# The stage between two mixtures of experts: sums on GpSimd, row copies on ScalarE, maxima as bias, attention products on two halves of the array

## The chip, the core and the metric

One core of one Trainium2 chip runs the whole program in one launch. The metric is the device time of that launch in microseconds (us), the median of several runs. One more execution was profiled; its span and its own time are given below. PE is TensorE, DVE is VectorE, ACT is ScalarE, POOL is GpSimd and SP is SyncE.

## What is computed

Four steps over x of 4 batches x 512 tokens x 512 features, all in float32. Only the third and the routing of the fourth lie in the stage that changes:

```python
x = x + L0_xattn(layernorm(x), ctx, ctx)          # 16 heads, 64 keys
x = x + L0_ffn(layernorm(x))                      # latent attention, then 1 shared + 7 routed experts, top 2
x = x + L1_xattn(layernorm(x), ctx, mask)         # one head of 512, 64 keys:
#   scores = x @ ctx.T * 512**-0.5; softmax over the keys that the mask keeps; attn @ ctx; zero if no key is kept
x = x + L1_ffn(layernorm(x))                      # softmax router over 32 experts, top 8, inner size 192
```

## The kernel before

The kernel has six stages, each a block in which the five engines run their own instruction lists and meet only at semaphores: `cross` (the first cross-attention), `front` (the latent attention and the first routing), `mixture` for MOE0, `middle` (from L1834), `mixture` for MOE1, and `finish`. Every engine works through its list in the order in which it is written, so an instruction that waits holds up all behind it on that engine.

`middle` reads the result of the first mixture from two tables in DRAM (`sum` and `other`) and adds them (`add_tables`, L2008). It works by batch (`BATCH` = 4) and in each by tile of 128 tokens (`TPB` = 4). For a batch b it does this:

- VectorE takes the statistics of each tile (`statistics`, L2013 to L2019) and GpSimd the power of -0.5 of the variance (`first_norm`, L1919). VectorE (batch 0, L2025) or ScalarE (L1942) writes the normed rows.
- TensorE flips them (`xn_flips`, L2174), ScalarE copies each flip out of PSUM (L1954), and TensorE makes the scores against the keys (`scores`, L2186).
- `softmax` on VectorE scales and masks the scores, takes the maximum and subtracts it (L2040 to L2043). ScalarE makes the exponents of all four tiles in one instruction (L1958). `shares` sums them, inverts the sum and multiplies (L2047 to L2051).
- `attended`: TensorE transposes the four tiles of 64 columns (L2193), ScalarE copies them (L1962), and TensorE multiplies each with the 64 rows of the context (L2198) into one of two banks of PSUM.
- `residual` on VectorE, tile by tile: it adds the product from PSUM to x (L2057) and takes the statistics of the sum (L2059); then aggregation and variance. The next product but one waits for the sum (`x3`). GpSimd makes the power (`second_norm`, L1923), VectorE the shift (`shift_of_hidden`, L2034), ScalarE the hidden rows (`hidden`, L1948).
- `logits`: TensorE flips the hidden rows, ScalarE copies them (L1968), TensorE multiplies with the router (L2213). VectorE subtracts the maximum (`shift_logits`), ScalarE exponentiates, `choose_experts` marks the eight best (L2076 to L2091).
- `run_keys` on TensorE (L2226, L2227), `run_starts` on VectorE (L2098 to L2101), then sixteen rounds of `pick` (L2107, L2109: the eight largest, then their replacement) and `list_runs` (L2113 to L2117) list the tokens of every expert. GpSimd writes the list to DRAM with four indirect DMAs, each of which waits for the last one (`write_runs`, L307).

The batches overlap by an order written out by hand. VectorE's loop for b runs: run starts and two picks of b-1, the hidden shift of b, seven picks, the softmax of b+1, seven picks and the list of b-1, the shares of b+1, the logits' shift and the choice of b, the residual of b+1. TensorE's loop: flips and scores of b+1, logits of b, two filler products (`keep_busy`, L212, results of no use), the attended products of b+1, the run keys of b. GpSimd's: second norm of b+1, run writes of b. SyncE first issues the loads in this order: context (L1889), the two tables for the first two tiles and for the next two (L1887), mask (L1892), tables of batch 1, router and run constants, tables of batches 2 and 3; then it stores the rows.

## Time and profile before

| what | us |
|---|---|
| median of 3 runs | 1802.04 |
| lowest and highest of them | 1789.2, 1822.32 |
| profiled execution, its own time | 1789.35 |
| its span | 1787.5 |
| PE, DVE, ACT, POOL busy | 1569.0, 1416.7, 1086.9, 793.5 |

### The profile page before, as it was taken

The numbers are of one execution on the slowest core, as the hardware profiler recorded it, in microseconds if no ns is written. First come the engines' busy times: TensorE is split into PE (matmuls) and PEld (weight loads), VectorE is DVE, ScalarE is ACT, GpSimd is POOL, SyncE is SP. The second block draws the span as 40 slices with busy tenths as digits, with TensorE's granted clock in tenths as the row PEclk, the third lists the DMA queues.
The fourth block names the chain that finished last, engine by engine and source line by source line (L and its number), as shares of the span: only waits on it lengthen the run. The fifth ranks groups of instructions, "written<-read, shape, count | busy, mean of one in ns | idle before, by whom it ended". The sixth has DMA issues, their size and how long they took to land. (4 is left out here: it accounts for less than half of the span.)

```text
span 1787.5 us, 34934 instructions
## 1 busy us (share of the span) xinstructions
PE 1569.0 (88%) x8910; PEld 1208.1 (68%) x8911; DVE 1416.7 (79%) x2889; ACT 1086.9 (61%) x2081; POOL 793.5 (44%) x547
## 2 busy tenths in 40 slices
PE   4578899998887899999959938999999999999990
PEld 2546666766564577777737526888888888888880
DVE  6835866867775488888748776999999999999992
ACT  1124644635452477888624316888888888888870
POOL 5010010110303323555410125788888888888871
PEclk9588998999999699999966658999999999999995
DMA  9225427354450644765574314988888889998768
GB/s 330 96 57 126 111 63 184 77 117 97 95 119 22 177 135 139 174 142 104 83 223 155 119 62 91 221 191 181 198 194 189 190 190 219 222 229 184 130 115 303
DMA packets 169999, 270.58 MB, mean 151 GB/s; under 512 B 20416, under 2 KB 96192, under 8 KB 168192
## 3 DMA queue, kind: packets, MB, share of 16 engines
q0 software_dynamic: 49008, 117.24, 32.7%
q1 hardware_dynamic: 120896, 152.18, 29.3%
q8 instruction: 46, 0.75, 0.2%
q14 instruction: 49, 0.40, 0.1%
HBM read 153.72 MB, written 89.06 MB: 136 GB/s over the span
## 5 line engine op out<-in xcount | busy, mean ns | idle before, releaser
L1662 DVE TENSOR_TENSOR moe_w_lo<-moe_w_up,moe_w_hi 128x1536 fp32r<-128x1536 f32 (+1 forms) x216 | 408.2, 1890 | 1.7 <-ACT moe_w_hi L1524 1.7
L1462 POOL DMA_INDIRECT moe_rows<-moe_rows,moe_ids x200 | 326.1, 1631 | 67.4 <-issue 57.9
L1524 ACT ACTIVATE moe_w_hi<-moe_w_up 128x1536 fp32r (+3 forms) x216 | 342.4, 1585 | 0.0
L1766 PE MATMUL psum<-moe_w_hi,moe_rows_hi 128*128 128x384 f32 (+1 forms) x864 | 322.5, 373 | 4.7 <-DVE moe_rows_lo L1656 4.7
L1767 PE MATMUL psum<-moe_w_lo,moe_rows_hi 128*128 128x384 f32 (+1 forms) x864 | 305.9, 354 | 0.0
L1768 PE MATMUL psum<-moe_w_hi,moe_rows_lo 128*128 128x384 f32 (+1 forms) x864 | 305.8, 354 | 0.0
L1776 PE MATMUL psum<-moe_w_down,moe_hid_t 128*128 (+1 forms) x432 | 221.3, 594 | 0.0
L1478 POOL DMA_INDIRECT moe_sum<-moe_res,moe_ids x100 | 163.2, 1632 | 81.3 <-ACT moe_res L1559 43.5
L1478 POOL DMA_INDIRECT moe_other<-moe_res,moe_ids x100 | 165.5, 1655 | 75.8 <-ACT moe_res L1559 33.6
L739 ACT ACTIVATE prob<-psum,neg_top 128x128 f32<-128x128 f32 (+3 forms) x256 | 133.1, 528 | 83.1 <-DVE neg_top L869 78.4
L1766 PEld LDWEIGHTS psum<-moe_w_hi,moe_rows_hi 128*128 128x128 f32 x864 | 163.4, 189 | 13.5 <-DVE moe_rows_lo L1656 5.8
L1768 PEld LDWEIGHTS psum<-moe_w_hi,moe_rows_lo 128*128 128x128 f32 x864 | 163.3, 189 | 9.4
L1767 PEld LDWEIGHTS psum<-moe_w_lo,moe_rows_hi 128*128 128x128 f32 x864 | 163.7, 189 | 7.9
L1656 DVE TENSOR_TENSOR moe_rows_lo<-psum,moe_rows_hi 128x512 fp32r<-128x512 f32 x216 | 149.1, 690 | 12.4 <-ACT moe_rows_hi L1507 6.0
L869 DVE TENSOR_REDUCE neg_top<-psum 128x1 f32<-128x128 f32 (+3 forms) x256 | 117.2, 482 | 50.0 <-PE psum L1093 49.8
L1546 ACT ACTIVATE moe_gate<-psum 128x192 f32<-128x192 f32 (+1 forms) x216 | 74.3, 344 | 134.6 <-PE psum L1768 134.5
L1507 ACT ACTIVATE moe_rows_hi<-psum 128x512 fp32r<-128x512 f32 x216 | 127.2, 589 | 21.7 <-PE psum L1747 21.7
L1134 PE MATMUL psum<-const_sb,prob 128*128 128x128 f32 x640 | 111.2, 289 | 29.7 <-ACT prob L739 26.6
L1747 PE MATMUL psum<-const_sb,moe_rows 128*128 128x128 f32 x864 | 130.0, 273 | 3.6 <-DMA moe_rows<-moe_rows,moe_ids 2.3
L1747 PEld LDWEIGHTS psum<-const_sb,moe_rows 128*128 128x128 f32 x864 | 107.5, 141 | 35.9 <-DMA moe_rows<-moe_rows,moe_ids 3.8
L1779 PE MATMUL psum<-moe_tail_hi,moe_tail_t 128*128 128x512 f32 x160 | 127.2, 795 | 0.0
L293 POOL DMA_INDIRECT moe_slots<-entry,slot x24 | 23.8, 992 | 231.9 <-DVE slot L992 225.5
(295 smaller groups left out, 3117.1 us busy)
## 6 DMA issues: line engine op xcount, KB each, us to landing
moe_w_up<-in_L_ffn_w_gate SPq DMA_DIRECT2D x32, 384.0 KB
moe_w_up<-in_L_ffn_w_up SPq DMA_DIRECT2D x32, 384.0 KB
q_st<-q_hi SPq DMA_DIRECT2D x64, 128.0 KB, 2.9
k_st<-k_hi SPq DMA_DIRECT2D x64, 128.0 KB, 3.0
k_st<-k_lo SPq DMA_DIRECT2D x64, 128.0 KB, 3.2
q_st<-q_lo SPq DMA_DIRECT2D x64, 128.0 KB, 3.0
moe_w_down<-in_L_ffn_w_down SPq DMA_DIRECT2D x32, 256.0 KB
moe_w_down<-in_L_ffn_w_down SPq DMA_DIRECT2D x64, 128.0 KB
```

What stands on the lines that cost most here:

```text
L739: sc.activation(prob[:, u, e, 0:(i + 1) * P], score_at(n, e, (i + 1) * P), ACT.Exp, bias=neg_top[:, u, e:e + 1], accum_out=den[:, i, 2 * h ...
L1462: pool.indirect_dma_start(rows[u][:, :], None, d["rows"], bass.IndirectOffsetOnAxis(ids[:, t:t + 1], 0)).then_inc(gathered[u], 16)
L1478: pool.indirect_dma_start(sums[t % 2], bass.IndirectOffsetOnAxis(ids[:, t:t + 1], 0), res[t % RESULTS][:, :], None, compute_op=ALU.add).th ...
L1507: sc.activation(rows_hi[i][:, :], ps[:, i, :], ACT.Copy).then_inc(T["rth"], 1)
L1524: sc.activation(w_hi[u % SPLITS][:, :], w_up[:, bass.ds(at * DC, DC), :].rearrange("p a n -> p (a n)"), ACT.Copy).then_inc(T["wh"], 1)
L1656: v.tensor_tensor(rows_lo[i][:, :], ps[:, i, :], rows_hi[i][:, :].bitcast(F32), ALU.subtract).then_inc(T["rts"], 1)
L1662: v.tensor_tensor(w_lo[u % SPLITS][:, :], w_up[:, bass.ds(at * DC, DC), :].rearrange("p a n -> p (a n)"), w_hi[u % SPLITS][:, :].bitcast(F ...
L1747: last = tr(ps[:, i, k * P:(k + 1) * P], rows[u][:, k * P:(k + 1) * P], ident)
L1766: mm(ps[:, 2 + i, 0:2 * I], hi, w_h, start=(k == 0), stop=False)
L1767: mm(ps[:, 2 + i, 0:2 * I], hi, w_l, start=False, stop=False)
L1768: last = mm(ps[:, 2 + i, 0:2 * I], lo, w_h, start=False, stop=(k == DC - 1))
L1776: mm(ps[:, 5 + i, :], hid_t[i][:, j, :], tile_at(w_down, at * n_fc + j), start=(j == 0), stop=False)
```

## The change

The sums of the two tables move to GpSimd for batches 1 to 3; batch 0 stays on VectorE, two tiles at a time. The residual sums move to GpSimd too: ScalarE copies each attended product from PSUM to `attended_sb`, and GpSimd adds that. The softmax no longer subtracts the maximum: VectorE writes it negated, and ScalarE takes it as the bias of four exponents, one a tile, which also give the sum. The context is loaded twice, into both halves of the partitions, and behind the first tables; two tiles of shares are transposed at once, so that even tiles lie in partitions 0 to 63 and odd ones in 64 to 127, and their products use the two halves of the array's rows. On VectorE the run starts and four rounds of picks of b come before the residual of b+1, two more behind it. Four semaphores of `front` are used again in `middle` and cleared for that at the start of the first mixture.

```diff
--- before
+++ after
...
+        m["spare_front"] = [S[n] for n in ("z", "zt", "zts", "pp")]
...
+            if moe is MOE0:
+                for used in m["spare_front"]:
+                    pool.sem_clear(used)
...
-        ctx_sb, ctx_t = sb("ctx_sb", [KEYS, BATCH, D]), sb("ctx_t", [P, BATCH, DC, KEYS])
+        ctx_sb, ctx_t = sb("ctx_sb", [P, BATCH, D]), sb("ctx_t", [P, BATCH, DC, KEYS])
...
-        att_t = sb("att_t", [KEYS, TPB, P])
+        att_t = sb("att_t", [P, TPB // 2, P])
+        attended_sb = sb("attended_sb", [P, TPB, D])
...
@@ SyncE @@
-            sp.dma_start(ctx_sb[:, :, :], a["ctx_2048"].rearrange("b k d -> k b d")).then_inc(S["ctx"], 16)
+            sp.dma_start(mask_u8[:, :, :].rearrange("p b k -> p (b k)"), a["mask_BxS2_bk0"].rearrange("b k -> (b k)").partition_broadcast(P)).then_inc(S["mask"], 16)
             tables(0, 2, x_in[0])
             tables(2, 2, x_in[1])
-            sp.dma_start(mask_u8[:, :, :].rearrange("p b k -> p (b k)"), a["mask_BxS2_bk0"].rearrange("b k -> (b k)").partition_broadcast(P)).then_inc(S["mask"], 16)
+            for half in range(2):
+                sp.dma_start(ctx_sb[half * KEYS:(half + 1) * KEYS, :, :], a["ctx_2048"].rearrange("b k d -> k b d")).then_inc(S["ctx"], 16)
@@ GpSimd @@
+            def residual(b):
+                for t in range(TPB):
+                    pool.wait_ge(attended_out, tile(b, t) + 1)
+                    at = x[:, tile(b, t), :]
+                    g.tensor_tensor(at, at, attended_sb[:, t, :], ALU.add).then_inc(S["x3"], 1)
+
             def second_norm(b):
+                residual(b)
                 pool.wait_ge(S["var2"], b + 1)
...
+            def add_tables(b):
+                pool.wait_ge(x_in[b + 1], 32)
+                for n in range(tile(b, 0), tile(b + 1, 0)):
+                    g.tensor_tensor(x[:, n, :], x[:, n, :], x_other[:, n, :], ALU.add).then_inc(added, 1)
+
             first_norm(0)
+            add_tables(1)
             first_norm(1)
+            add_tables(2)
+            add_tables(3)
             second_norm(0)
@@ ScalarE @@
-                act.wait_ge(S["shift"], b + 1)
-                sc.activation(att[:, :, :], att[:, :, :], ACT.Exp).then_inc(S["e"], 1)
+                act.wait_ge(S["ntop"], b + 1)
+                for t in range(TPB):
+                    sc.activation(att[:, t, :], att[:, t, :], ACT.Exp, bias=top[:, t:t + 1], accum_out=den[:, t:t + 1]).then_inc(S["e"], 1)
...
-                sc.activation(att_t[:, :, :].rearrange("p t q -> p (t q)"), ps[0:KEYS, 5, :], ACT.Copy).then_inc(S["pts"], 1)
+                sc.activation(att_t[:, :, :].rearrange("p t q -> p (t q)"), ps[:, 5, 0:TPB // 2 * P], ACT.Copy).then_inc(S["pts"], 1)
+
+            def attended_rows(b):
+                for t in range(TPB):
+                    act.wait_ge(S["o"], tile(b, t) + 1)
+                    since(act, S["x3"], tile(b - 1, t) + 1)
+                    sc.activation(attended_sb[:, t, :], ps[:, 6 + t % 2, :], ACT.Copy).then_inc(attended_out, 1)
...
@@ VectorE @@
+            def add_tables(t):
+
+                if t % 2 == 0:
+                    dve.wait_ge(x_in[t // 2], 32)
+                own.did(v.tensor_tensor(x[:, t, :], x[:, t, :], x_other[:, t, :], ALU.add))
...
+                else:
+                    for t in range(TPB):
+                        dve.wait_ge(added, tile(b - 1, t) + 1)
+                        own.did(v.bn_stats(stats[:, t, :], x[:, tile(b, t), :]))
...
-                own.run(v.tensor_reduce(top[:, :], att[:, :, :], AX.X, ALU.max))
-                v.tensor_tensor(att[:, :, :], att[:, :, :], top[:, :].unsqueeze(2).to_broadcast([P, TPB, KEYS]), ALU.subtract).then_inc(S["shift"], 1)
+                v.tensor_reduce(top[:, :], att[:, :, :], AX.X, ALU.max, negate=True).then_inc(S["ntop"], 1)
...
-                dve.wait_ge(S["e"], b + 1)
-                own.run(v.tensor_reduce(den[:, :], att[:, :, :], AX.X, ALU.add))
+                dve.wait_ge(S["e"], TPB * (b + 1))
...
-                    dve.wait_ge(S["o"], tile(b, t) + 1)
-                    at = x[:, tile(b, t), :]
-                    v.tensor_tensor(at, at, ps[:, 6 + t % 2, :], ALU.add).then_inc(S["x3"], 1)
                     dve.wait_ge(S["x3"], tile(b, t) + 1)
-                    own.did(v.bn_stats(stats2[:, t, :], at))
+                    own.did(v.bn_stats(stats2[:, t, :], x[:, tile(b, t), :]))
...
-                if b > 0:
-                    run_starts(b - 1)
-                    pick(b - 1, range(0, 2))
                 shift_of_hidden(b)
                 if b == 0:
                     statistics(2)
                 else:
-                    pick(b - 1, range(2, 9))
+                    pick(b - 1, range(6, 9))
...
                 shift_logits(b)
                 choose_experts(b)
                 if ahead:
+                    run_starts(b)
+                    pick(b, range(0, 4))
                     residual(b + 1)
+                    pick(b, range(4, 6))
@@ TensorE @@
-                for t in range(TPB):
-                    last = tr(ps[0:KEYS, 5, t * P:(t + 1) * P], att[:, t, :], ident)
+                for j in range(TPB // 2):
+                    last = tr(ps[:, 5, j * P:(j + 1) * P], att[:, 2 * j:2 * j + 2, :].rearrange("p t k -> p (t k)"), ident)
...
-                    since(pe, S["x3"], tile(b, t) - 1)
-                    mm(ps[:, 6 + t % 2, :], att_t[:, t, :], ctx_sb[:, b, :], start=True, stop=True).then_inc(S["o"], 1)
+                    since(pe, attended_out, tile(b, t) - 1)
+                    rows = slice(t % 2 * KEYS, (t % 2 + 1) * KEYS)
+                    mm(ps[:, 6 + t % 2, :], att_t[rows, t // 2, :], ctx_sb[rows, b, :], start=True, stop=True).then_inc(S["o"], 1)
...
-            pe.wait_ge(S["ctx"], 16)
+            pe.wait_ge(S["ctx"], 32)
```

## Rows read from the trace of the kernel before

**Rows 1.** Busy time by stretch of the stage; columns: us, each engine's busy us, PEclk, DMA share, GB/s

```profile
904.17:946.06 41.89, 32.21 (x110) 18.66 (x111) 25.42 (x61) 10.29 (x16) 3.06 (x3) 0.66 0.68 234
946.06:971.38 25.32, 23.18 (x117) 16.01 (x117) 22.27 (x78) 11.30 (x20) 3.02 (x3) 0.77 0.46 139
971.38:1005.25 33.87, 33.19 (x119) 24.36 (x119) 23.81 (x101) 11.76 (x20) 5.01 (x5) 0.51 0.59 185
1005.25:1031.39 26.14, 23.78 (x106) 13.34 (x104) 23.50 (x99) 7.00 (x13) 4.95 (x5) 0.75 0.30 107
1031.39:1060.36 28.97, 11.08 (x53) 9.83 (x52) 24.61 (x121) 5.39 (x9) 3.91 (x4) 0.56 0.16 54
```

**Rows 2.** Timeline of TensorE in the round of 33.9 us: start, duration, engine, line, operation

```profile
960.19 7.19 PE L2198 MATMUL psum<-m_ctx_sb,m_att_t 64*128 64x512 f32 x8 [0.72 <-ACT m_att_t L1962]
...
968.19 3.81 PE L2174 MATMUL psum<-const_sb,m_xn 128*128 128x128 f32 x16
...
971.79 6.93 PE L2186 MATMUL psum<-m_ctx_t,m_xn_t 128*128 128x64 f32 x32
...
988.72 3.68 PE L212 MATMUL psum<-const_sb 128*64 128x512 f32 x4
```

**Rows 3.** Groups of VectorE in the stage: count | busy us, mean ns of one | idle before

```profile
L2107 DVE MAX8 m_picks<-m_left 128x8 f32<-128x128 f32 x60 | 17.6, 294 | 1.9
L2109 DVE MATCH_REPLACE8 m_left<-m_picks,m_left 128x128 f32<-128x128 f32 x56 | 15.4, 275 | 0.0
...
L2059 DVE BATCH_NORM_STATS2 m_stats<-m_x_sb 128x6 f32<-128x512 f32 x16 | 11.1, 694 | 0.6
...
L2057 DVE TENSOR_TENSOR m_x_sb<-m_x_sb,psum 128x512 f32<-128x512 f32 x16 | 10.9, 682 | 5.5 <-PE psum L2198 5.2
...
L2008 DVE TENSOR_TENSOR m_x_sb<-m_x_sb,m_x_other 128x512 f32<-128x512 f32 x16 | 10.1, 686 | 19.6 <-DMA m_x_other<-moe_other 19.6
...
L2047 DVE TENSOR_REDUCE m_den<-m_att 128x4 f32<-128x256 f32 x4 | 1.7, 413 | 2.3 <-ACT m_att L1958 2.3
```

**Rows 4.** Groups of GpSimd and ScalarE by shape: prices of what is moved to them

```profile
L719 POOL TENSOR_TENSOR x_sb<-x_sb,h 128x512 f32<-128x512 f32 x16 | 20.0, 1264 | 202.7 <-DVE h L955 186.3 <-DMA moe_slots<-entry,slot 16.4
...
L739 ACT ACTIVATION_READ_ACCUMULATOR prob<-psum,neg_top 128x1 f32 x256 | 52.2, 204 | 0.0
...
L1954 ACT ACTIVATE m_xn_t<-psum 128x512 f32<-128x512 f32 x16 | 9.4, 597 | 31.8 <-PE psum L2174 31.8
...
L1958 ACT ACTIVATE m_att<-m_att 128x256 f32<-128x256 f32 x4 | 1.7, 415 | 1.8 <-DVE m_att L2043 1.8
```

**Rows 5.** Timeline of the lead-in: context, filler products, table sums, first attended product

```profile
909.33 1.97 PE L2219 MATMUL psum<-const_sb,m_ctx_sb 64*128 64x64 f32 x16 [13.64 <-DMA m_ctx_sb<-in_ctx]
...
911.23 6.77 PE L212 MATMUL psum<-const_sb 128*64 128x512 f32 x10
...
911.88 1.29 DVE L2008 TENSOR_TENSOR m_x_sb<-m_x_sb,m_x_other 128x512 f32<-128x512 f32 x2 [18.16 <-DMA m_x_other<-moe_other]
...
914.59 1.29 DVE L2008 TENSOR_TENSOR m_x_sb<-m_x_sb,m_x_other 128x512 f32<-128x512 f32 x2 [1.41 <-DMA m_x_other<-moe_other]
...
937.33 5.38 PE L2198 MATMUL psum<-m_ctx_sb,m_att_t 64*128 64x512 f32 x8 [0.68 <-ACT m_att_t L1962]
...
938.56 0.69 DVE L2057 TENSOR_TENSOR m_x_sb<-m_x_sb,psum 128x512 f32<-128x512 f32 x1 [0.19 <-PE psum L2198]
```

**Rows 6.** Timeline of GpSimd: first and last of four run writes of batch 0

```profile
986.60 1.05 POOL L307 DMA_INDIRECT moe_slots<-m_run_ids,run_at  x1 [16.05 <-DVE m_run_ids L2117]
...
995.13 0.96 POOL L307 DMA_INDIRECT moe_slots<-m_run_ids,run_at  x1 [1.98 <-DMA moe_slots<-m_run_ids,run_at]
```

**Rows 7.** A line of GpSimd with its shortest, median and longest ns; VectorE's timeline beside it

```profile
L410 POOL TENSOR_TENSOR c_x_rest<-c_x_rest,c_mean x9: 1254/1265/2237, 27.3 to 38.7; 128x512 f32<-128x512 f32 x9
...
36.36 1.23 DVE L474 TENSOR_TENSOR c_att<-c_att,const_sb 128x1024 f32<-128x1024 f32 x1
...
38.88 2.13 DVE L476 TENSOR_TENSOR c_att<-c_att,c_top 128x1024 f32<-128x1024 f32 x1
```

More of the change, by code:

```diff
@@ L1846, in middle @@
         ps, x = m["psum"], sb("x_sb", [P, TILES, D])
[L1847 to L1848 removed]
+        ctx_sb, ctx_t = sb("ctx_sb", [P, BATCH, D]), sb("ctx_t", [P, BATCH, DC, KEYS])
+        N, K, spare = MOE1.routed, MOE1.top, m["spare"] + m["spare_front"]
         w_rt = sb("w_rt", [P, DC, N])
@@ L1871, in middle @@
         run_ids = [sb(f"run_ids{u}", [P, P]) for u in range(BATCH - 1)] + [m["run_ids"]]
-        names = ("w mask ctx ct cts xn ft fe s shift e p pt pts o x3 hn logit lsh le masked ranked "
+        names = ("w mask ctx ct cts xn ft fe s ntop e p pt pts o x3 hn logit lsh le masked ranked "
                  "slotted rows_out own var rstd var2 rstd2 shared runs shift1 shift2").split()
@@ L2117, in list_runs @@
                 v.tensor_tensor(run_ids[b][:, :], found[:, :], empty[:, :], ALU.add).then_inc(S["slotted"], 1)
-            add_tables(0)
-            statistics(0)
-            normed(0)
             dve.wait_ge(S["mask"], 16)
@@ L2126, in _ @@
             own.wait()
-            add_tables(1)
+            statistics(0)
+            normed(0)
             statistics(1)
```

26 lines of the change are left out of this document (11 added, 15 removed).

## Prediction

> **What bounds the kernel now.** I read the busy time by stretch first [rows 1]. The stretch of the change, the stage between the mixtures, is 904.2 to 1060.4, 156 us of the span of 1787.5, so whatever happens there is small against the whole. I cut it where the shift of the second norm of a batch is written (L2034), since everything of the next batch hangs on that point; call it T(b). T(0) to T(3) are 946.06, 971.38, 1005.25 and 1031.39, so there are a lead-in of 41.9 us, rounds of 25.3, 33.9 and 26.1, and a tail of 29.0. The columns to compare are DVE, PE and the clock. In the round of 26.1 DVE works 23.5, and with the gap of some 0.03 after each of its 99 instructions that is all of it: VectorE bounds it. In the round of 33.9 the granted clock is 0.51, the lower level (1.2 GHz), PE is busy 33.2 and DVE only 23.8: there TensorE's own queue is the bound. TensorE's timeline of that round [rows 2] shows that queue: attended products from 960.19 (7.2), then the run keys, flips and scores of the next batch (3.8 and 6.9), flips and logits from 978.5 to 988.8, two filler products (3.7), transposes and a copy, and then the next attended products. So a round is the later of two loops, and the clock decides which.
>
> **The change, part by part.**
> *VectorE.* What goes are twelve of sixteen table sums at 0.686, sixteen residual sums at 0.682, four reductions of 128x256 at 0.413 and four subtractions of that size, put at 0.42 [rows 3]: 8.2 + 10.9 + 1.7 + 1.7 = 22.5 us. Half of it lies in the lead-in and first round. In a later round 2.73 + 0.42 + 0.41 = 3.6 go, and VectorE alone would need 26.1 - 3.6 = 22.5.
> *What takes its place.* A residual row now goes TensorE, ScalarE copy out of PSUM (0.597 for 128x512), GpSimd sum, VectorE statistics (0.694) [rows 3, 4]. The same sum of 128x512 on GpSimd stands in the attention stage: 1.264 [rows 4]. Four in a row are 5.05, and the last statistics come some 0.72 after them. Before, sum and statistics took 1.38 a tile, 5.5 for four: with 1.23 from the first product to what reads it (937.33 to 938.56, [rows 5]) it was 6.7 at the high clock. The new chain is no shorter: 1.23 + 0.65 + 5.05 + 0.72 = 7.65.
> *Exponents.* One of 128x256 at 0.415 becomes four of 128x64 with an accumulated sum. The read of an accumulator is 0.204 [rows 4]; the small exponent itself has no row, it lies between 0.1 (a quarter) and 0.415; I take 0.26, so 4 x (0.26 + 0.204) + gaps = 1.95, 1.5 longer. It sits on ScalarE between the second and third copy of the hidden flips, hence on the path to the logits, partly.
> *Two halves of the array.* Two transposes of 128x128 instead of four with 64 columns, and an att_t copy of half the length: 0.5 less. Products of even and odd tiles use different rows. A pair takes 3.4 at the low clock now; side by side it would take 1.7, one after the other 3.4, and the trace has no pair on row halves. I take side by side: some 2.4 less a batch at the low clock, 1.2 at the high one. The Trainium skill ("TensorEngine Tiling (Array Packing)", Key Properties) says that different tiles of the array run LdWeights and Matmul in parallel; no run shown bears that out for these halves, and by the other end a low round would be about 2 longer.
> *Lead-in.* The context comes last now and twice (1 MB), behind the first two table pairs. Those arrive at 911.88 and 914.59, 1 MB in 2.7 us [rows 5]; without 0.5 MB ahead of them they come 1.35 earlier, and the context at 913.2 + 2.7 = 915.9 instead of 909.3. TensorE's queue is in order: 16 transposes 2.0, ten filler products 6.8 [rows 5], so the flips of batch 0 start at 924.7 though the normed rows come no later than now. Flips and scores are 10.7 at the low clock [rows 2]; the high one gives between half of it and that, I take 7.5: scores at 932.2 (935.4 if low). Softmax without its subtraction 1.4, the load of the exponent's table, unchanged, put at 1.3, exponents 1.95, shares without the reduction 0.9, transposes and copy 0.95: products at 938.7; at the low clock the filler products behind the scores, eight passes of the 0.68 of [rows 5], end at some 942 and put them 3.5 later. GpSimd has its twelve table sums done by about 939.0: batch 1 lands at 921.5 (2 MB more at the rate above), its four sums end 926.6, batches 2 and 3 follow the norm at 928.9 (8 x 1.264). First attended row at 938.7 + 1.23 + 0.65 = 940.6, sums to 945.65, statistics, aggregation and variance 1.3, norm and shift 1.45: T(0) = 948.4, which is 2.3 late.
> *First round.* Hidden rows 3.0, two copies 1.2, exponents 2.0, two copies 1.2, last logits 1.0: 956.8; filler 1.85 (half of the 3.7), transposes, copy: products at 960.0. Now a new wait decides. VectorE goes to the run starts before the residual statistics, and the run keys stand behind the attended products in TensorE's queue. At the high clock they are there at 964.0, else 966.4, while VectorE is through choosing at 961.3. Run starts 0.55 and four rounds of picks (maximum 0.294, replacement 0.275, its load and gaps: 0.72 each, [rows 3]) 2.85, four statistics 2.9, then 0.6 and 1.25: T(1) = 972.1 or 974.5, against 971.38.
> *Later rounds, high clock.* GpSimd's queue decides. The residual sums of batch b+1 stand behind the run writes of batch b-1, four indirect DMAs that each wait for the last one: issued 986.60 to 996.09 [rows 6], 9.5; the chains of the other batches look a little shorter, I take 9.1. Before, only a 1 us power stood behind them. The ids are ready at T + 0.2 + 2.15 + 1.4 + 4.65 + 1.2 = T + 9.6 (three picks, softmax, seven picks, the list). So the writes end at T + 19.0, the sums at 24.05, statistics at 24.8, and with 0.6 and 1.15 the round is 26.5. VectorE's 22.5 is no longer the bound and the round is 0.4 longer, not 3.6 shorter.
> *Later rounds, low clock.* TensorE's loop of 33.9 less 2.4 (pairs) and 0.5 + 0.2 (transposes, copy), plus 1.2 for the wait of the second pair on the copies: about 32.0.
> *Contention.* A GpSimd sum beside a two-input VectorE instruction took 2.237 instead of 1.265, and that instruction (L476) 2.13 where the same size just before (L474) took 1.23 [rows 7]: each pays 0.9. In the residuals GpSimd works beside picks and statistics, which have one SBUF input; only the two softmax operations and the shares of batch 0 meet table sums, with 1 us of slack. I price it at 0 and keep +2 as its end. The Trainium skill ("GPSIMD Engine Reference", the table of the engine's properties) names this contention for VectorE instructions with two SBUF inputs; by the rule the trace agrees, and it would only matter if picks paid it too.
> *Cleared semaphores.* Four more at the start of the first mixture. No row shows a clear. An indirect issue on GpSimd takes 0.96 [rows 6], so four clears lie between 0 and 3.8; I take 0.4, near the lower end, since a clear moves nothing.
>
> **The sum.** With the clock as in this trace (round 1 low, round 2 high, tail unchanged at 29.0): 974.5 + 32.0 + 26.5 + 29.0 = 1062.0, against 1060.4: 1.6 later, and 0.4 makes 2.0. The profiled execution took 1789.35 beside its span of 1787.5, so its like would take 1791.4. The three timed runs stand higher, 1789 to 1822 with median 1802.0; the trace does not show why, and on that scale the sum is 1804.0. I forecast the middle of the two, 1798, which puts no change at 1796. What a measurement of this kernel tells from no change is about 2%, 36 us.
>
> **Rivals.**
> 1. VectorE's 22.5 us come off whole, because every round is VectorE's. For: the busy shares of rounds 0 and 2. Against: the low clock in round 1 and GpSimd's order. Time: 1796 - 22.5 = 1773.5, some 1774. Chance 0.07.
> 2. The clock stays high through the rounds: 972.1 + 2 x 26.5 + 29.0 = 1054.1, 6.3 earlier, less the 0.4: 1790. For: TensorE waits on VectorE less. Against: the five stretches of now stand at 0.51 to 0.77. Chance 0.25.
> 3. Slower: the run keys' wait at the low clock in both rounds. VectorE stands before the residual statistics until TensorE is through its products. It decides where round 2 falls to 1.2 GHz: 974.5 + 64 + 29 = 1067.5, 7.1 later plus 0.4, and 3.5 where the lead-in is low too: 1796 + 11 = 1807. With products one after the other and contention it is 2 x 2 + 2 more, 1813. Chance 0.25.
> 4. The change does not do what it says: pairs serial and four exponents at their upper end (0.62 each, 0.6 more a round than I took, for three rounds, and 2 a round for the pairs): 8 later, 1806. Chance 0.08.
> My forecast has the other 0.35. Every case lies inside 2%; the 0.06 outside is the spread of the runs.
>
> **Range and chances.** The cases span 1774 to 1813, and the runs of one kernel alone differ by 33. I give 1780 to 1818. Over 2% faster would need under 1766, below what even rival 1 gives: 0.03. Over 2% slower, above 1838: 0.03. Within: 0.94.
>
> **What would show it.** Right: the stage from the first context DMA to the end of the last list at 152 to 164 us; VectorE's busy time in it down from 119.6 to about 97, with new idle before the run starts (now L2098) and before the residual statistics; GpSimd sums of 1.26 that begin right behind the fourth run write in batches 2 and 3; flips of batch 0 not before 924. Wrong: statistics that follow the copies at once, context transposes before 914, a stage under 145 or over 170, or a difference that lies outside the stage.

## The result, and the profile after

Four runs of the changed kernel have the median 1818.3 us (1806.6 to 1829.9), beside 1799.6 of four runs of the kernel before. The ratio is 1.0119 [1.0068, 1.017], in brackets the 95% interval: about 21 us slower, 12 to 31. A ratio is estimated from the runs that are not in the chip's slower state, and is not the quotient of the two medians (those differ by 18.7). The prediction, 1798 with 1780 to 1818, said no change; the median lies just above the upper end. The profiled execution took 1818.0 beside its span of 1816.2.

First the busy time by stretch of the changed kernel, cut at the same points as [rows 1] (its stage begins at 916.04, the hidden shift is L2070; us, then PE, PEld, DVE, ACT and POOL busy, PEclk, DMA share, GB/s):

```profile
916.04:965.93 49.89, 27.80 (x131) 16.44 (x131) 20.30 (x47) 13.95 (x28) 23.20 (x19) 0.71 0.65 207
965.93:993.04 27.11, 21.67 (x126) 15.61 (x124) 19.65 (x81) 14.13 (x30) 7.99 (x7) 0.87 0.60 191
993.04:1025.13 32.09, 26.52 (x112) 20.42 (x112) 23.46 (x95) 14.24 (x30) 9.95 (x9) 0.65 0.53 159
1025.13:1057.33 32.20, 20.28 (x74) 13.39 (x73) 23.80 (x93) 9.27 (x22) 9.86 (x9) 0.66 0.21 76
1057.33:1086.64 29.31, 11.51 (x52) 10.89 (x52) 22.02 (x108) 5.39 (x9) 3.90 (x4) 0.50 0.14 47
```

The stage takes 170.6 us, before 156.2. The lead-in is 8.0 longer (49.9 against 41.9), the first round 1.8 longer, the second 1.8 shorter, the third 6.1 longer, the tail 0.3 longer. What follows the stage takes 729.6, before 727.1. The stage also starts 11.9 later, in code that is the same but for four clears; the runs below show that this part moves by itself. So 14.4 of the 28.7 us between the two profiles lie in the stage; against a second execution of the kernel before, whose stage took 146.9 (experiment 5), it is 23.7 longer. A stage over 170, and a difference outside it, were among the signs that I had named of being wrong. Note the DVE column: 109.2 us in the sum, not the 97 that was forecast, though the sums did leave; 7.5 of the 12 are one copy, as the next view shows.

The second view says why; these are groups of VectorE, GpSimd and ScalarE in the stage of the changed kernel (count | busy us, mean ns of one | idle before), to hold against [rows 3, 4]:

```profile
L2138 DVE MAX8 m_picks<-m_left 128x8 f32<-128x128 f32 x60 | 17.6, 294 | 1.8
L2090 DVE BATCH_NORM_STATS2 m_stats<-m_x_sb 128x6 f32<-128x512 f32 x16 | 10.2, 685 | 7.1 <-POOL m_x_sb L1932 7.0
L2130 DVE COPY before<-before 128x32 f32<-128x32 f32 x4 | 8.2, 2046 | 0.0
L2129 DVE COPY m_base<-psum 128x1 f32<-128x1 f32 x4 | 0.6, 158 | 13.5 <-PE psum L2255 13.5
...
L1932 POOL TENSOR_TENSOR m_x_sb<-m_x_sb,m_attended_sb 128x512 f32<-128x512 f32 x16 | 19.8, 1268 | 10.5 <-ACT m_attended_sb L1991 10.5
L1942 POOL TENSOR_TENSOR m_x_sb<-m_x_sb,m_x_other 128x512 f32<-128x512 f32 x12 | 15.1, 1295 | 5.0 <-DMA m_x_other<-moe_other 5.0
...
L1991 ACT ACTIVATE m_attended_sb<-psum 128x512 f32<-128x512 f32 x16 | 8.7, 594 | 9.7 <-PE psum L2226 9.7
L1981 ACT ACTIVATE m_att<-m_att,m_top 128x64 f32<-128x64 f32 x16 | 5.4, 338 | 0.4 <-DVE m_top L2078 0.3
```

A copy of 128x32 has a mean of 2046 ns. Where no sum of GpSimd runs beside it, it takes 0.17 us. And VectorE stands 13.5 us before the line ahead of it, for the run keys. The maxima and statistics have the durations of before, and GpSimd's sums are the 1.26 that [rows 4] showed.

Where that copy stands is plain in the second round, in the timelines of GpSimd and VectorE of the changed kernel (start, us, engine, line):

```profile
1002.41 1.05 POOL L307 DMA_INDIRECT moe_slots<-m_run_ids,run_at  x1 [9.77 <-DVE m_run_ids L2148]
...
1011.50 0.96 POOL L307 DMA_INDIRECT moe_slots<-m_run_ids,run_at  x1 [2.01 <-DMA moe_slots<-m_run_ids,run_at]
1012.49 4.96 POOL L1932 TENSOR_TENSOR m_x_sb<-m_x_sb,m_attended_sb 128x512 f32<-128x512 f32 x4
```

```profile
1008.90 0.29 DVE L2122 TENSOR_TENSOR m_share<-m_share,m_r_total 128x128 f32<-128x128 f32 x1
1013.76 0.16 DVE L2129 COPY m_base<-psum 128x1 f32<-128x1 f32 x1 [4.57 <-PE psum L2255]
1013.84 3.65 DVE L2130 COPY before<-before 128x32 f32<-128x32 f32 x1
1017.53 0.22 DVE L2132 SCALAR_TENSOR_TENSOR run_at<-m_runs,m_base 128x4 int32<-128x4 f32 x1
...
1020.54 2.47 DVE L2090 BATCH_NORM_STATS2 m_stats<-m_x_sb 128x6 f32<-128x512 f32 x4
```

The four residual sums begin right behind the fourth run write, as forecast, and run from 1012.49 to 1017.45. VectorE comes free at 1009.2, waits 4.6 for the run keys, starts its copy (L2130) 1.35 after the sums began, and the copy ends at 1017.49, with the last of them. Only then come four rounds of picks and the statistics, so the shift is written 7.7 after the last sum. In the third round the copy takes 4.14 (from 1045.56), again to the end of the sums.

Last the lead-in of the changed kernel, to hold against [rows 5]:

```profile
923.60 1.29 DVE L2036 TENSOR_TENSOR m_x_sb<-m_x_sb,m_x_other 128x512 f32<-128x512 f32 x2 [1.80 <-DMA m_x_other<-moe_other]
928.47 1.29 DVE L2036 TENSOR_TENSOR m_x_sb<-m_x_sb,m_x_other 128x512 f32<-128x512 f32 x2 [2.25 <-DMA m_x_other<-moe_other]
...
945.27 1.23 DVE L2066 SCALAR_TENSOR_TENSOR m_shift<-m_mv,m_rstd 128x4 f32<-128x4 f32 x1 [1.13 <-POOL m_rstd L1926]
946.62 0.42 DVE L2076 SCALAR_TENSOR_TENSOR m_att<-psum,m_mask 128x256 f32<-128x256 f32 x1
947.09 0.90 DVE L2077 TENSOR_TENSOR m_att<-m_att,m_barred 128x256 f32<-128x256 f32 x1
...
952.84 1.44 DVE L2085 TENSOR_TENSOR m_att<-m_att,m_den 128x256 f32<-128x256 f32 x1
```

```profile
932.32 1.97 PE L2247 MATMUL psum<-const_sb,m_ctx_sb 64*128 64x64 f32 x16 [24.11 <-DMA m_ctx_sb<-in_ctx]
934.22 6.37 PE L212 MATMUL psum<-const_sb 128*64 128x512 f32 x10
940.51 1.09 PE L2201 MATMUL psum<-const_sb,m_xn 128*128 128x128 f32 x8
...
955.25 2.08 PE L2226 MATMUL psum<-m_ctx_sb,m_att_t 64*128 64x512 f32 x4 [0.47 <-ACT m_att_t L1985]
958.00 2.56 PE L2226 MATMUL psum<-m_ctx_sb,m_att_t 64*128 64x512 f32 x4 [0.68 <-ACT m_attended_sb L1991]
```

Counted from the stage's start, the context is transposed at 16.3 (before 5.2), the flips of batch 0 start at 24.5 (before 16.6), the first attended product at 39.2 (before 33.2), and from there to the shift it takes 10.7 (before 8.7). The shift, the masking and the shares of batch 0 are each held by GpSimd's table sums: 1.23, 0.90 and 1.44, where later batches need 0.16, 0.43 and 0.43.

### The profile page after: what moved, and what is told of

Same layout as the page of the kernel before. It is cut to its first block and busy times, and to the rows that moved or that the text cites. A ratio compares the mean times of both kernels' runs of the same rounds, so it can differ in the third digit from the quotient of the medians.

```text
span 1816.2 us, 34972 instructions
## 1 busy us (share of the span) xinstructions
PE 1561.9 (86%) x8902; PEld 1206.9 (66%) x8903; DVE 1407.1 (77%) x2853; ACT 1098.5 (60%) x2125; POOL 829.1 (46%) x575
## 5 line engine op out<-in xcount | busy, mean ns | idle before, releaser
L1770 PEld LDWEIGHTS psum<-moe_w_hi,moe_rows_hi 128*128 128x128 f32 x864 | 163.6, 189 | 14.4 <-DVE moe_rows_lo L1660 6.6
L1550 ACT ACTIVATE moe_gate<-psum 128x192 f32<-128x192 f32 (+1 forms) x216 | 74.3, 344 | 134.8 <-PE psum L1772 123.5
L293 POOL DMA_INDIRECT moe_slots<-entry,slot x24 | 23.7, 987 | 234.8 <-DVE slot L993 228.4
```

Of the source, the lines that this page charges most:

```text
L1770: mm(ps[:, 2 + i, 0:2 * I], hi, w_h, start=(k == 0), stop=False)
```

## The experiments

My theory after this profile: the loss is the residual on GpSimd, by its place in two queues and by the held instructions, and a smaller loss is the lead-in. The rivals: the late context and table loads, the tables on GpSimd, or the clock. Eleven variants were run, and the kernel before once more. "A" is the changed kernel, "B" the kernel before; all ratios are to the kernel before. A profile is one execution, so a stage or round is one sample; `...` in the diffs marks what is left out.

**1. Another instruction in the place of the held copy** (on A):

```diff
-                own.did(v.tensor_copy(before[:, 0, :], before[:, TPB, :]))
+                own.did(v.tensor_reduce(before[:, 0, :], before[:, TPB, :].unsqueeze(2), AX.X, ALU.add))
```

> The changed kernel with one VectorE instruction replaced: the copy of the last row of before to the first is a reduction over an axis of length one, same result. In the changed kernel that copy took 3.65 and 4.14 us in the second and third round, and both ended when GpSimd's four residual sums ended. Contention theory: a copy of f32 from SBUF to SBUF is held while GpSimd adds, a reduction is not: it takes 0.2, the run starts and the four picks move 3 to 4 us earlier, the statistics follow the last sum, and each of the two rounds is 2.5 to 3.5 us shorter; stage 170.6 to about 165. Rival (the wait for the run keys alone delays the statistics): the operation behind it is held in the same way or nothing hangs on it, and the rounds stay at 32.

Measured: 1816.3 us, ratio 1.0124 [1.0029, 1.022]; stage 168.6, not 165, and the two rounds are 32.2 and 33.0, not shorter. VectorE's timeline in the third round of this kernel, where the sums run from 1031.86 to 1036.78:

```profile
1033.52 0.16 DVE L2129 COPY m_base<-psum 128x1 f32<-128x1 f32 x1 [4.32 <-PE psum L2255]
1033.60 0.18 DVE L2130 TENSOR_REDUCE before<-before 128x32 f32<-128x32 f32 x1
1033.81 3.01 DVE L2132 SCALAR_TENSOR_TENSOR run_at<-m_runs,m_base 128x4 int32<-128x4 f32 x1
```

The reduction passes in 0.18 and the next instruction is held in its stead, to the end of the sums. So it is the kind of instruction that is held, not the place in the program, and swapping one kind moves the hold by one line. The second round says something else, and it matters: there the granted clock is 0.50 and the run keys come only at 1003.25, 24.3 after the shift. Reduction and scalar_tensor_tensor take 0.18 and 0.24, nothing is held, and the round is still 32.2, since run starts and picks stand ahead of the statistics. Late run keys, with TensorE busy 29.9 of the 32.2, make such a round without any hold.

**2. VectorE's order of before** (on A): statistics first, then the run starts and two picks.

```diff
-                    pick(b - 1, range(6, 9))
+                    pick(b - 1, range(2, 9))
...
+                    residual(b + 1)
                     run_starts(b)
-                    pick(b, range(0, 4))
-                    residual(b + 1)
-                    pick(b, range(4, 6))
+                    pick(b, range(0, 2))
```

> The changed kernel with VectorE's order of before: residual statistics right after the choice of experts, then run starts and two picks, seven more behind the hidden shift. Head-of-line theory (VectorE stands before the run keys and then before GpSimd, with the statistics behind it): statistics follow each sum, the shift comes 2.7 after the last sum instead of 7.6, rounds two and three 4 to 5 us shorter, the copy takes its 0.17 again since GpSimd is through; stage about 160. Rival (the run writes ahead of the sums on GpSimd bound the round): only 1 to 2 us a round.

Measured: 1820.5 us, ratio 1.0125 [1.0034, 1.0216]. The copies take 0.17, the shift follows the last sum by 3.3 (1048.89 to 1052.16) instead of 7.7, and still the later rounds are 31.2 and 30.7. In the third round the last run write ends 22.5 after the shift (1043.94 - 1021.43), where in A it was 19.6: the ids come later now, and the sums behind the writes with them. 4.4 gained, 2.9 given back, 1.5 left in that round. The stage is 161.2 all the same, 9.4 shorter than in A: 6.1 of this is the first round (21.0, where A has 27.1), in which the run starts and four rounds of picks no longer stand ahead of the residual statistics. The whole time does not show it; its interval is two per cent wide.

**3. The context first, the mask last** (on A), the preparation of the mask behind the first normed rows:

```diff
+            for half in range(2):
+                sp.dma_start(ctx_sb[half * KEYS:(half + 1) * KEYS, :, :], ...
-            sp.dma_start(mask_u8[:, :, :]...
             tables(0, 2, x_in[0])
             tables(2, 2, x_in[1])
+            sp.dma_start(mask_u8[:, :, :]...
```

> The changed kernel with the order of loads of before: both halves of the context first, then the tables, mask last of these, and the mask's preparation again behind the normed rows. Load theory: the context arrives some 8 us earlier than 16.3 after the stage's start, the flips of batch 0 start 4 to 6 us earlier than 24.5, lead-in 49.9 to about 46. Rival (GpSimd's table sums and their contention bound the lead-in): the first tables come 2 to 4 us later and the lead-in stays at 49 to 51.

Measured: 1810.1 us, ratio 1.0092 [1.004, 1.0144]. The stage is 165.9, the lead-in 48.4, only 1.5 shorter. The scores are there 25.3 after the start instead of 30.5, but VectorE takes them at 28.7: it stands in order behind batch 1, and so behind GpSimd's table sums. The timelines of VectorE and GpSimd of this kernel:

```profile
925.92 1.36 DVE L2153 CAST m_mask<-m_mask_u 128x256 f32<-128x256 uint8 x1
927.32 1.25 DVE L2154 TENSOR_SCALAR m_barred<-m_mask 128x256 f32<-128x256 f32 x1
928.49 0.41 DVE L2155 TENSOR_REDUCE m_any_key<-m_mask 128x4 f32<-128x256 f32 x1
...
933.16 1.22 DVE L2066 SCALAR_TENSOR_TENSOR m_shift<-m_mv,m_rstd 128x4 f32<-128x4 f32 x1 [1.13 <-POOL m_rstd L1926]
```

```profile
924.45 5.25 POOL L1942 TENSOR_TENSOR m_x_sb<-m_x_sb,m_x_other 128x512 f32<-128x512 f32 x4 [1.45 <-DMA m_x_other<-moe_other]
```

The cast and the subtraction took 0.29 each in A, where no sum stood beside them; here 1.36 and 1.25. The reduction between keeps its 0.41. So the late loads were not the main cause of the longer lead-in, and waiting for GpSimd takes most of the gain.

**4. The sums ahead of the run writes** (on A):

```diff
                 second_norm(b + 1)
-                write_runs(pool, m, b, run_ids[b][:, :], r1["slots"], S["slotted"])
+                if b > 0:
+                    write_runs(pool, m, b - 1, run_ids[b - 1][:, :], r1["slots"], S["slotted"])
+            write_runs(pool, m, BATCH - 2, run_ids[BATCH - 2][:, :], r1["slots"], S["slotted"])
```

> The changed kernel with GpSimd's residual sums of a batch ahead of the run writes that stand before them now. By the prediction's step on GpSimd's queue the sums start when the first attended row is copied: at 1011.6 instead of 1012.5 and 1043.3 instead of 1044.7, so no more than 1 to 1.5 us a round; stage 168 to 170. If the run writes had cost more than the trace shows, 3 or more a round.

Measured: 1814.4 us, ratio 1.0087 [1.0035, 1.0139]. The stage is 166.2, the later rounds 30.9 and 30.9 at a granted clock of 0.61 and 0.67: 1.2 and 1.3 less than in A, as expected. The sums now begin when the first attended row is copied, but in the second round that is 19.8 after the shift (TensorE is at the lower level and busy 27.5 of 30.9), and the order of VectorE puts the shift 6.2 behind the last sum. Neither 2 nor 4 alone frees the later rounds.

**5. The parts alone on the kernel before.** Halves of the array, with both context loads first:

```diff
-                for t in range(TPB):
-                    last = tr(ps[0:KEYS, 5, t * P:(t + 1) * P], att[:, t, :], ident)
+                for j in range(TPB // 2):
+                    last = tr(ps[:, 5, j * P:(j + 1) * P], att[:, 2 * j:2 * j + 2, :].rearrange("p t k -> p (t k)"), ident)
...
-                    mm(ps[:, 6 + t % 2, :], att_t[:, t, :], ctx_sb[:, b, :], ...
+                    mm(ps[:, 6 + t % 2, :], att_t[rows, t // 2, :], ctx_sb[rows, b, :], ...
```

> The kernel before with one part of the change alone: context in both halves of the partitions (loaded first, as now), two transposes, products of odd tiles on the other half of the array. Theory from the changed kernel's TensorE timeline (four products of a pair group in 1.13 us where two of them took 1.7 at the low clock): a round at the low clock is 2.5 to 3.5 us shorter than 33.9, one at the high clock unchanged, since VectorE bounds it; lead-in 1 to 2 longer for the second context load; stage 150 to 157. Rival (nothing gained since VectorE's residual, 1.38 a tile, is as slow as the products): stage 156 to 159.

Measured: 1795.9 us, ratio 0.9955 [0.9912, 0.9998]. It is the one part whose interval lies below 1, and that by 0.0002, so this is a hint and no proof of a gain. The stage is 149.6, with later rounds of 26.0 and 25.7, PE busy 100.7 us in the stage where B had 123.5 and, in another execution (below), 109.0.

The residual alone (ScalarE copies, GpSimd sums, all orders as before):

```diff
+                    sc.activation(attended_sb[:, t, :], ps[:, 6 + t % 2, :], ACT.Copy).then_inc(attended_out, 1)
...
+                    g.tensor_tensor(at, at, attended_sb[:, t, :], ALU.add).then_inc(S["x3"], 1)
...
-                    v.tensor_tensor(at, at, ps[:, 6 + t % 2, :], ALU.add).then_inc(S["x3"], 1)
```

> The kernel before with the residual sums on GpSimd and the ScalarE copies alone, VectorE's order unchanged. Theory: the chain product, copy, sum, statistics costs 2 us a batch more than the sums on VectorE (10.7 against 8.7 from the first product to the shift in the lead-in), and the sums of batches 2 and 3 stand behind the run writes; stage 158 to 164. Rival (VectorE was the bound and gets 2.7 us a round back): 150 to 155.

Measured: 1814.3 us, ratio 1.0086 [1.0027, 1.0144], most of the whole loss; stage 164.7. Its third round, at a granted clock of 0.71 with flips, scores and logits at the higher level, shows the mechanism undisturbed; GpSimd's timeline of this kernel, then VectorE's:

```profile
1025.72 1.02 POOL L307 DMA_INDIRECT moe_slots<-m_run_ids,run_at  x1 [13.98 <-DVE m_run_ids L2128]
...
1034.37 0.96 POOL L307 DMA_INDIRECT moe_slots<-m_run_ids,run_at  x1 [1.75 <-DMA moe_slots<-m_run_ids,run_at]
1035.35 4.92 POOL L1927 TENSOR_TENSOR m_x_sb<-m_x_sb,m_attended_sb 128x512 f32<-128x512 f32 x4
```

```profile
1029.91 0.29 DVE L2102 TENSOR_TENSOR m_share<-m_share,m_r_total 128x128 f32<-128x128 f32 x1
1036.65 0.69 DVE L2070 BATCH_NORM_STATS2 m_stats<-m_x_sb 128x6 f32<-128x512 f32 x1 [6.45 <-POOL m_x_sb L1927]
1037.87 0.69 DVE L2070 BATCH_NORM_STATS2 m_stats<-m_x_sb 128x6 f32<-128x512 f32 x1 [0.52 <-POOL m_x_sb L1927]
```

The first attended row was copied at 1029.37, the sums begin at 1035.35, when the four writes are through. VectorE stands 8.0 us in this round for them (6.45 and three times 0.52), and the round is 31.0 where the same order without the move has 26.1 to 26.3. No copy is held here (0.17 each), so the 4.7 to 4.9 are the new chain and its queue; experiment 6 tells them apart.

The table sums of batches 1 to 3 alone:

```diff
+            def add_tables(b):
+                pool.wait_ge(x_in[b + 1], 32)
+                for n in range(tile(b, 0), tile(b + 1, 0)):
+                    g.tensor_tensor(x[:, n, :], x[:, n, :], x_other[:, n, :], ALU.add).then_inc(added, 1)
```

> The kernel before with the table sums of batches 1 to 3 on GpSimd alone. Theory: in the lead-in VectorE waits for GpSimd's four sums (4.9 against 2.5 us, begun when batch 1 has landed) and its two-port instructions are held meanwhile, so the first attended product comes 2 to 5 us later than 33.2 us after the start; the first round gets up to 2.5 back that VectorE spent on batch 3; stage 156 to 161. Rival (loads set the lead-in, the sums do not): lead-in stays at 42, stage 153 to 156.

Measured: 1801.2 us, ratio 0.9974 [0.9929, 1.002]. The stage is 152.8, below both ranges. The lead-in is 47.9 (held instructions, granted clock 0.61), and the first attended product comes at 37.4 instead of 33.2, as the theory had it. The first round, now without table sums on VectorE, is 22.3. Against [rows 1] it returns 3.0 of the 6.1 lost; against the second execution of B below (42.9 and 23.5), 1.2 of 5.1. The whole shows no loss.

The kernel before once more, one execution:

> The kernel before once more, for its own spread. Theory: the stage's length follows the granted clock of its rounds, and the profile that I have happened to get a round at the high clock; a second one gives a stage between 152 and 164 us, and a start of the stage that differs by several us from 904, since the stages ahead vary in both kernels. Rival: stage 156 within 1 us and start at 904, so that all 28.7 us of the two profiles belong to the change.

Measured: 1804.7 us, span 1802.8. Its stage takes 146.9, not 156.2, and less than the 152 I gave as the lower end. The stretches of its second and third round:

```profile
983.00:1009.34 26.34, 21.62 (x99) 13.23 (x99) 23.68 (x101) 10.28 (x18) 5.00 (x5) 0.75 0.60 189
1009.34:1035.61 26.27, 23.35 (x107) 14.18 (x106) 23.46 (x99) 7.19 (x13) 4.95 (x5) 0.76 0.46 160
```

The round of 33.9 in [rows 1] is 26.3 here: the clock at 0.51 belonged to that execution. And the span is 15 longer although the stage is 9 shorter: it starts at 916.7 instead of 904.2, and what follows takes 739.2 instead of 727.1. Over fourteen profiled executions of eleven variants and both kernels those two parts move between 898.6 and 920.3, and between 726.5 and 743.5, without regard to the edit. So stages are compared with stages, and the 11.9 us ahead of the changed stage are not the change's.

The maxima as bias alone:

```diff
-                sc.activation(att[:, :, :], att[:, :, :], ACT.Exp).then_inc(S["e"], 1)
+                for t in range(TPB):
+                    sc.activation(att[:, t, :], att[:, t, :], ACT.Exp, bias=top[:, t:t + 1], accum_out=den[:, t:t + 1]).then_inc(S["e"], 1)
...
-                own.run(v.tensor_reduce(top[:, :], att[:, :, :], AX.X, ALU.max))
-                v.tensor_tensor(att[:, :, :], att[:, :, :], top[:, :].unsqueeze(2)..., ALU.subtract).then_inc(S["shift"], 1)
+                v.tensor_reduce(top[:, :], att[:, :, :], AX.X, ALU.max, negate=True).then_inc(S["shift"], 1)
```

> The kernel before with the maxima as bias alone: the negated maximum goes to ScalarE as the exponent's bias, four exponents of 64 columns add up their own sums; a subtraction and a reduction leave VectorE. Theory A: four exponents take 1.3 us where one took 0.42, VectorE loses 0.84 us a batch, rounds at high clock 25.5 us instead of 26.3, the time 0 to 4 us lower, ratio 0.997 to 1.000. Rival: the four exponents delay the second shares by 0.9 us a batch and nothing is won, ratio 1.000 to 1.003.

Measured: 1786.9 us, ratio 1.0007 [0.9967, 1.0048]; stage 148.3. The second round is 25.3 at a granted clock of 0.77, 1.0 shorter than the 26.3 at 0.75 above, and the whole shows nothing: a few tenths of a per cent are below what these runs tell.

**6. Both orders together** (edits 2 and 4 on A):

> The changed kernel with two edits together: GpSimd adds the attended rows of a batch ahead of the previous batch's run writes, and VectorE does the statistics of the hidden rows first, then the run starts and two picks, so that nothing of VectorE's stands beside GpSimd's sums but the statistics. Theory A (the cost of the residual on GpSimd is its place in two queues): the run writes no longer delay the sums (in the variant with only the residual moved, high-clock round 31.0, VectorE idle 8.0 us in it for the sums, 4.7 us more than the 26.3 of the kernel before), the copy takes 0.17 us and no operation is held to the end of the sums; a round at high clock takes 26 to 27 us, and the time is 1.004 of before or less (what is left is the lead-in, some 6 us). Rival B (the rounds of these kernels are long since TensorE stays at its low clock): rounds again 30 to 31 us at a granted clock of 0.6 to 0.67, and the ratio is 1.008 to 1.012 as with either edit alone.

Measured: 1798.5 us, ratio 1.0036 [1.0001, 1.0072]. The stretches of this kernel:

```profile
900.92:951.39 50.47, 27.80 (x123) 16.45 (x124) 20.42 (x47) 13.96 (x28) 23.19 (x19) 0.68 0.64 205
951.39:972.37 20.98, 17.74 (x106) 13.45 (x105) 16.36 (x69) 14.23 (x30) 7.98 (x7) 0.87 0.55 166
972.37:1002.53 30.16, 26.78 (x126) 21.52 (x126) 20.22 (x95) 14.37 (x31) 6.61 (x6) 0.69 0.57 175
1002.53:1028.58 26.05, 18.18 (x89) 11.12 (x88) 20.04 (x94) 9.15 (x22) 10.02 (x10) 0.87 0.39 137
```

This is the test of the theory. With the sums neither behind the run writes nor beside anything that they hold, the stage is 157.0 instead of 170.6, and some two thirds of the loss are gone (0.0036 of 0.0119 is left). The first round gives 6.1 of the 13.6, the third 6.2, the second 1.9. In the third round, GpSimd's timeline and then VectorE's:

```profile
1020.38 4.94 POOL L1932 TENSOR_TENSOR m_x_sb<-m_x_sb,m_attended_sb 128x512 f32<-128x512 f32 x4 [5.07 <-ACT m_attended_sb L1993]
```

```profile
1021.68 0.69 DVE L2092 BATCH_NORM_STATS2 m_stats<-m_x_sb 128x6 f32<-128x512 f32 x1 [2.39 <-POOL m_x_sb L1932]
```

The sums begin 17.9 after the shift, where the residual alone had 22.8, and the round is 26.05, where that kernel had 31.0. The flips (eight in 1.04) and the logits' products (eight in 1.08) run at the higher level in both, so the clock does not make the difference of 4.9. Nor do the halves and the bias that only this kernel has: in the other the first row lay ready 16.8 after the shift, here at 17.7, and it was the writes that it waited 6.0 for. It is the place behind the run writes. The chain over two more engines costs little in its place, about the 1.2 by which the third round of experiment 7 is shorter. Yet VectorE is busy only 20.0 in the round: the 3.6 us that left it still buy nothing, since it then waits 4.0 for the sums (2.39, 0.54, 0.53 and 0.53). Against A the comparison is less clean, since A's third round stands at 0.66 and this one at 0.87. What is left of the loss lies in the lead-in (50.5) and in the second round (30.2 at 0.69).

**7. The residual back on VectorE** (on A, in the order of 2, run writes where A has them):

```diff
             def second_norm(b):
-                residual(b)
...
             attention_out(0)
-            attended_rows(0)
...
+                    v.tensor_tensor(at, at, ps[:, 6 + t % 2, :], ALU.add).then_inc(S["x3"], 1)
```

> The changed kernel with its residual part undone: VectorE adds the attended rows from PSUM itself, in the order of the kernel before; ScalarE copies none, GpSimd adds only the tables. Theory A (the residual on GpSimd carries the loss, the tables on GpSimd and the late context a smaller one in the lead-in): rounds of 25.7 to 26.5 us where the clock is high, lead-in 47 to 50 us, stage 152 to 156 us, ratio 0.997 to 1.004. Rival B (the tables on GpSimd and the loads carry as much): stage over 160 us, ratio 1.008 or more.

Measured: 1784.9 us, ratio 1.0007 [0.9967, 1.0047]. Stretches of 48.2, 21.8, 25.9, 24.8 and 29.3, stage 150.0. Tables on GpSimd, the late context, the bias, the halves and the clears are all still in it. Against 6 it is 6.9 us shorter, in the lead-in (2.2), the second round (4.3) and the third (1.2); only the first round is 0.8 longer.

**8. The best of the parts** (on B): halves and bias, tables and residual on VectorE, the second context copy behind batch 1's tables with its own semaphore.

```diff
+            sp.dma_start(ctx_sb[KEYS:P, :, :], a["ctx_2048"].rearrange("b k d -> k b d")).then_inc(ctx_low, 16)
...
                 pe.wait_ge(S["pts"], b + 1)
+                pe.wait_ge(ctx_low, 16)
```

> The kernel before with the two halves of the array and the maxima as bias, tables and residual left on VectorE, and the context's second copy loaded behind batch 1's tables, with a semaphore of its own that only the products wait for. Theory A: the first context load lands as early as before (T(0) about 42 us after the stage's start, where the variant with both copies first had 45.5), rounds of 25 to 25.5 us at high clock; stage 144 to 147 us, time 1788 to 1794 us, ratio 0.992 to 0.996. Rival: the second copy delays the tables of batches 2 and 3 or the clock falls in the rounds, and the ratio is 0.997 to 1.000.

Measured: 1781.9 us, ratio 0.9973 [0.9941, 1.0006]. The lead-in is 44.5, one us better than with both copies first, not the 42 I expected; the stage is 148.8. It is no clear gain over the kernel before.

## Why the prediction was wrong

**The step that failed** is the later round: "the writes end at T + 19.0, the sums at 24.05, statistics at 24.8, and with 0.6 and 1.15 the round is 26.5". The sums themselves came as forecast, to 0.6 us: in the second round they run from T + 19.45 to T + 24.4, in the third from 19.6 to 24.5. A part of that is luck: my terms (9.6 and 9.1) add up to T + 18.7, not 19.0, and in the second round the list was ready at 9.1 and the writes took 10.05. But I let run starts and four rounds of picks pass on VectorE while GpSimd adds. They pass only where the run keys are early, and where the copy is not held. I had worked out that wait for the first round and left it out of the later ones. Here the keys come late: VectorE begins the run starts 1.3 and 0.8 after the sums began, its copy is held to their end, and picks and statistics all come behind. From the last sum to the shift it is 7.7 instead of 2.45, and the rounds are 32.1 and 32.2. With nothing in between, as in experiments 2 and 6, it is 3.3, so 4.4 of it is the order and the hold, and 0.8 was short in any case. The stage ended 12.8 later than the sum had it: 5.7 are the third round, 5.7 the lead-in, 1.0 the first round.

**The second step** is the contention ("I price it at 0"), since GpSimd works beside "picks and statistics, which have one SBUF input". These indeed pay nothing (0.29 and 0.69 beside sums, experiments 1 and 6). I overlooked the 128x32 copy ahead of the picks: it has one input too and takes 3.65 and 4.14 instead of 0.17. Two-input instructions were not the whole class: copy, cast and tensor_scalar from SBUF to SBUF are in it (experiment 3). What [rows 7] showed, each pays 0.9, was not found here either: GpSimd's four sums took 4.96 and 4.92, as if alone, and VectorE paid all (beside the table sums of experiment 3 GpSimd did pay a little, 5.25). The Trainium skill has it ("SBUF — State Buffer", Who interferes with whom): the port pair is an exclusive lock, and copy, cast and tensor_scalar can take it; I had gone by the line that the prediction cites. By its rule the holder keeps the lock for one instruction; the trace agrees where the held instruction took 0.9 to 1.4, but the copy was held through three sums in a row, and through the rest of one and three more, so here the measurement goes further than the page.

**The lead-in** was 2.3 late by my sum and 8.0 in the trace. Several terms were short. The second table pair is added 12.4 after the start, not 9, and the context transposed at 16.3, not 11.7, so flips start at 24.5, not 20.5; the high clock gave 1.5 of it back, and the scores end at 30.5, 2.5 later than my 28.0. Then 8.7 instead of 6.5 pass to the first product, of which VectorE's holds are 0.1, 0.5 and 1.0; another 1.0 is the exponent's table load behind ScalarE's normed rows of batch 1, which had waited for the held shift, and the exponents gave 0.5 back. And from product to shift it is 10.7 instead of 9.7. Experiment 3 shows that earlier loads bring back only 1.5 of this; 7 against 6, that the residual chain is 2.2 of it.

**The clock.** I took the clock of one execution as the pattern, low in the second round, high in the third. The second execution of B shows 0.75 and 0.76. The low round of before, 33.9, was thus no fixed gain to be had. That the second round came out at 32.1 where I forecast 32.0 is luck: I had it bound by TensorE's queue, but PE is busy only 26.5 of it, and it is the wait and the hold above that fill it. Against the other execution of B, 26.3, it is a loss.

**The rivals.** The third, slower by VectorE's wait ahead of the statistics, named the place: rounds of 32 and 32 and a tail of 29. It gave 1807, with the stage 11 us longer; measured are 14.4, and what it lacked is mainly the lead-in (2.2 more than with its 3.5) and the first round (1.0 more). I gave it 0.25. Its condition was met in the main: both rounds stand at 0.65 and 0.66, with the logits at the lower level. It had no held copy in it, but the second round of experiment 1 shows that at 0.50 the late keys make 32.2 without one; in A's rounds both are at work. How the order of A does in a later round at the higher level throughout, no run shows. The first rival, 22.5 us off, is refuted by experiment 6: VectorE's time did go, its wait took the place. The second did not come, and the fourth's conditions did not hold.

**Right** were the sums right behind the fourth write, their duration, the order of events on GpSimd, the side-by-side products (a pair in 1.13 at the higher level, 2.08 at the lower, where a pair took 3.4), and the flips of batch 0 not before 924. The small exponents were priced too high: four with their accumulator reads take 1.44 us (950.77 to 952.21), not 1.95.

**Open.** Why the clock falls in one execution and not in the next, and so how much of the 4.3 between 6 and 7 in the second round is the edit's: both stand at 0.69, yet PE is busy 26.8 in the one and 22.9 in the other. The four clears were not tried by themselves; kernels 6 and 7 have them and start the stage at 900.9 and 903.3, no later than B. How much of the whole time experiment 2 or 4 gains alone is open too: their intervals are one to two per cent wide and overlap with A's, while their profiled stages are 9.4 and 4.4 shorter.

## What to carry to other kernels

Before work is moved to an idle engine, write down its queue there: which instructions stand ahead, what they wait for, and when the moved one could start at the earliest. Here three DMA writes at a distance of 2.6 to 3.5 us and a fourth stood ahead of it, and 3.6 us off the busy engine became 4 to 8 us of waiting (experiments 6 and 5). Where GpSimd and VectorE both work in SBUF, mark every copy, cast, scalar and two-input form that could fall beside a run of GpSimd's instructions, however small: it can last as long as the rest of the run. In VectorE's own list, put what waits for a late event behind what is on the path to the next batch: here the run starts stood before the statistics. And profile the kernel before twice: one execution's low clock is not a property of the code.

## What the hardware showed that was not expected

- A VectorE copy of 128x32 that takes 0.17 alone waited until three or four GpSimd sums in a row were over (3.65 and 4.14 us); a scalar_tensor_tensor of 128x4 did the same (3.01). Elsewhere the holds were about one sum each: beside the table sums 1.23 for 0.16, 1.36 for 0.29, 1.44 for 0.43, and beside the residual sums of A's first round (981.92 to 986.87, four in a row) 0.22 for the copy and 1.18 for the scalar_tensor_tensor behind it. So neither the kind of instruction nor that of the sums decides it; what does is open.
- Maximum, replacement, statistics, reductions and instructions that read PSUM beside one SBUF input kept their durations beside sums (0.29, 0.28, 0.69, 0.41, 0.42).
- The context's second copy, 0.5 MB into 64 partitions, cost as much as 1 MB of tables into 128. With both copies ahead (experiment 3) the first table sum comes 10.3 after the stage's start instead of 7.7, 2.6 later; a table pair of 1 MB takes 2.7 [rows 5]. While the copies and then the first tables load, the rate is 218 GB/s, with tables alone 368. That the 64 partitions are the reason is not shown: no run loads the same bytes in both ways. These are the two rows, of the kernel of experiment 3 and of the kernel before:

```profile
906.00:914.70 8.70, 1.42 (x13) 1.42 (x14) 0.00 (x0) 0.27 (x1) 0.00 (x0) 0.50 0.88 218
```

```profile
909.40:914.60 5.20, 5.20 (x20) 2.68 (x21) 1.30 (x3) 1.19 (x2) 0.00 (x0) 0.50 1.02 368
```

- An exponent of 128x64 takes 0.338 and its accumulator read 0.19, but they overlap: one pair every 0.33.
